# The seventh batch's norm, choice and places moved behind the last scores, the start reordered, two batches' sends two steps earlier

## The reference

```python
x = x + attn_a(layernorm(x))   # x: 8 x 256 x 128; 16 heads of 64, relative bias, full rows
x = x + ffn(layernorm(x))      # router over 8 experts, top 1
x = x + attn_b(layernorm(x))   # 64 x 32 tokens, low-rank keys and values, causal
x = x + ffn(layernorm(x))
# ffn:
router_logits = xt @ Wr + br
gates = max(softmax(router_logits)); idx = argmax(softmax(router_logits))
h = relu(layernorm(xt)*ln_g + ln_b through W1[idx] + b1[idx])
y = (h through W2[idx] + b2[idx]) * gates
```

## Time and profile before

| | |
|---|---|
| median of 3 runs | 656.47 us (655.35 to 656.65) |
| the profiled execution | 655.51 us |
| its span, first to last instruction | 654.2 us |
| mean granted clock of TensorE | 0.997 of 2.4 GHz |
| TensorE busy | 629.4 us, 96% |
| VectorE busy | 513.5 us, 78% |
| ScalarE busy | 529.0 us, 81% |
| GpSimd busy | 355.7 us, 54% |

### The profile page before, as it was taken

One profiled execution on the slowest core, in us unless ns is written; L12 is line 12 of the kernel. 1 busy time (PEld: TensorE's weight loads), 2 busy tenths in 40 slices (PEclk: granted clock), 3 DMA queues, 4 the chain that ended last, 5 costly groups with the idle time before them and its releaser, 6 DMA issues.

```text
span 654.2 us, 22111 instructions
## 1 busy us (share of the span) xinstructions
PE 629.4 (96%) x7454; PEld 537.3 (82%) x7454; DVE 513.5 (78%) x2211; ACT 529.0 (81%) x1776; POOL 355.7 (54%) x669
## 2 busy tenths in 40 slices
PE   6899999999999999989999999999999999989997
PEld 5578788788878788779997788888888888878997
DVE  4886878778987888988856687787888789888833
ACT  3888888879788878785665998898989898985664
POOL 4463545455465556743106564565657665762746
PEclk9999999999999999999999999999999999998999
DMA  8999989999980000133631100000000000112140
GB/s 271 284 321 326 273 229 326 330 329 289 286 238 10 11 2 26 42 100 91 168 96 37 34 3 3 8 2 7 6 7 19 12 11 2 50 52 74 49 132 19
DMA packets 90319, 74.78 MB, mean 114 GB/s; under 512 B 12225, under 2 KB 87111, under 8 KB 90080
## 3 DMA queue, kind: packets, MB, share of 16 engines
q1 hardware_dynamic: 86512, 66.24, 34.9%
q0 software_dynamic: 2848, 6.33, 3.0%
q10 hardware_dynamic: 848, 0.79, 0.5%
HBM read 19.93 MB, written 54.00 MB: 113 GB/s over the span
## 4 chain that ended last, share of the span: by engine, by line
PE 82%; issue 4%; DVE 4%; ACT 4%; POOL 3%; DMA 1%; SPq 0%; DVEq 0%; ACTq 0%; POOLq 0%
PE ps L558 17%; PE ps L671 14%; PE ps L715 13%; PE ps L553 10%; PE ps L554 8%; PE ps L555 8%; PE ps L821 5%; PE ps L837 5%; ACT ring L1020 2%; POOL out L439 1%; POOL ring L419 1%; DVE ring L1335 1%; DMA wkn<-in_w_qkv 1%; POOL xs_scratch L406 1%; PE ps L771 1%
## 5 line engine op out<-in xcount | busy, mean ns | idle before, releaser
L419 POOL TENSOR_SCALAR ring<-ring,rs 128x256 f32<-128x256 f32 (+1 forms) x500 | 218.8, 456 | 132.3 <-DVE rs L1347 130.9
L1020 ACT ACTIVATE ring<-ring,mn 128x256 f32<-128x256 f32 (+1 forms) x512 | 243.5, 482 | 5.8 <-DVE mn L1335 5.7
L558 PE MATMUL ps<-ident,ring 128*128 128x128 f32 x896 | 121.8, 275 | 4.8 <-DVE ol L1307 2.5
L558 PEld LDWEIGHTS ps<-ident,ring 128*128 128x128 f32 x896 | 102.0, 143 | 13.5 <-issue 4.7
L671 PE MATMUL ps<-qk 64*64 64x256 f32 (+1 forms) x2048 | 112.3, 356 | 0.6 <-ACT qk L992 0.4
L715 PE MATMUL ps<-pt,v 64*64 64x256 f32 (+3 forms) x2048 | 103.5, 340 | 1.5 <-ACT pt L1008 1.5
L1020 ACT ACTIVATION_READ_ACCUMULATOR ring<-ring,mn 128x1 f32 x512 | 101.3, 198 | 0.0
L715 PEld LDWEIGHTS ps<-pt,v 64*64 64x64 f32 x2048 | 75.3, 134 | 28.2 <-ACT pt L1008 6.0
L1362 DVE COPY pt<-ps 128x512 f32<-128x512 f32 (+1 forms) x128 | 75.5, 590 | 22.4 <-PE ps L558 21.0
L671 PEld LDWEIGHTS ps<-qk 64*64 64x64 f32 x2048 | 65.8, 132 | 29.0 <-issue 11.4
L992 ACT COPY qk<-ps 128x512 f32<-128x512 f32 x128 | 74.3, 580 | 9.9 <-PE ps L555 9.8
(11 more groups left out here) (209 smaller groups left out, 1298.0 us busy)
## 6 DMA issues: line engine op xcount, KB each, us to landing
xs_scratch<-f_ys SPq DMA_DIRECT2D x16, 2064.0 KB, 20.5
yr_scratch<-f_ys SPq DMA_DIRECT2D x8, 1024.0 KB, 10.6
f_xs<-xs_scratch SPq DMA_DIRECT2D x50, 129.0 KB, 2.3
w<-in_W SPq DMA_DIRECT2D x16, 256.0 KB, 5.9
xs_scratch<-f_ys SPq DMA_DIRECT2D x2, 1677.0 KB, 19.9
yr_scratch<-f_ys SPq DMA_DIRECT2D x25, 64.0 KB, 1.8
T<-in_bias SPq DMA_DIRECT2D x2, 512.0 KB, 7.9
T<-in_bias SPq DMA_DIRECT2D x1, 1024.0 KB, 10.4
```

The lines of the kernel that those rows point to most:

```text
L419: i = pool.tensor_scalar(part, part, rs[:, q], 1.0, ALU.mult, ALU.mult)
L558: return pe.transpose(out, src, ident[:, :])
L1020: i = act.activation(part, part, ACT.Exp, bias=mn[:, q], scale=-1.0, accum_out=sm[:, q])
```

## The change

Batch 6 leaves the common table and gets NEXT_POST: its sums stand in step 64 in place of 61, its logits and choice in 68, its places in 70; batch 7 keeps its steps 68 to 72. At the start of stage 1 ScalarE makes the value weights ahead of T(1) and does T(2) ahead of the first exponential; VectorE does products(3) and the norm of batch 1 in step 2, behind the first four scores, and its transposes come in step 5; GpSimd turns the bias tables a step off from before. Batches 1 and 3 are put up for sending before the step's send and not after it, so their first send comes one even step earlier. In step 63 VectorE does keep(58) between the reciprocal and the product of weigh(61), and index(4) behind S(63). The core of the diff:

```diff
+SENDS = {56: 2, 59: 2, 60: 2}
+BIASES = {1: 2, 2: 4, 4: 6}
+FIRST_PRE = {"a": 2, "a2": 4, "b": 5}
+NEXT_POST = {"sums": 64, "pow": 64, "a": 65, "xn": 65, "b": 66, "c": 68, "lg": 68, "choose": 68, "gate": 69, "d": 69, "place": 70}
...
+    if s == NEXT_POST[part]:
+        return NB - 2
     b = at(s, POST[part])
-    return b if b is not None and CALM <= b < NB - 1 else None
+    return b if b is not None and CALM <= b < NB - 2 else None
...
-            for _ in range(2 if s > 56 else 1):
-                if to_send and s <= NU and (s % 2 == 0 or s > 56):
+            if (b := calm_post(s, "place")) in ROUTED:
+                to_send.extend((j, ROUTE_NO[b], b) for j in range(*ROUTED[b]))
+            for _ in range(SENDS.get(s, 1 - s % 2)):
+                if to_send and s <= NU:
                     send()
-            for b in either(s, "place"):
-                to_send.extend((j, ROUTE_NO[b], b) for j in range(*ROUTED.get(b, (0, 0))))
+            if (b := post_at(s, "place")) in ROUTED:
+                to_send.extend((j, ROUTE_NO[b], b) for j in range(*ROUTED[b]))
                 while to_send and b >= NB - 2:
                     send()
...
+            if st == 0 and s == 1:
+                value_weights()
             if 0 <= s < NU:
                 T(s)
+            if s == 2:
+                expo(0, ALL[0])
             if st == 0 and s == 1:
-                value_weights()
                 products(3)
...
-                if s in (NU - 3, NU - 1):
+                if s == NU - 3:
                     weigh(s - 2)
                 if s == NU - 1:
+                    weigh(s - 2, (0,))
                     keep(NU - 6)
+                    weigh(s - 2, (1,))
                     TR(NU - 4)
                     TR(NU - 3)
+                S(s)
+                if s == NU - 1:
                     index(4)
-                S(s)
...
+            if s == NEXT_POST["sums"]:
+                sums(NB - 2)
+            if s == NEXT_POST["a"]:
+                post_a(NB - 2)
+                post_a2(NB - 2)
```

More of the change, by code:

```diff
@@ L104, in pre_at @@
         return 0 if st else None
+    if not st and part in FIRST_PRE:
+        if s == FIRST_PRE[part]:
+            return 1
+        if at(s, PRE[part]) == 1:
+            return None
     if st and s == PRE_1.get(part):
@@ L454, in step @@
                 weigh(s - 3)
-            if st == 0 and s in (1, 3, 5):
-                biases(s + 1)
-            if (b := pre_at(s + 1 if st and s < 0 else s - 1, "a", st)) is not None and (b or s < 0) and not (st and b == 1):
+            if st == 0 and s in BIASES:
+                biases(BIASES[s])
+            if st == 0 and s == FIRST_PRE["a"]:
+                pool_pow(rstd, half[:, 0:2], v_var0, p_pow0, 2)
+            if (b := pre_at(s + 1 if st and s < 0 else s - 1, "a", st)) is not None and (b or s < 0) and b != 1:
                 if st and b == 0:
@@ L758, in post_b @@
         def post_b(b):
-            PX = spare(("p", B0 + b), a_pTs, B0 + b + 1)
+            PX = spare(("p", B0 + b), a_pTs, B0 + b + 1, 3 if b == NB - 2 else None)
             pe.wait_ge(v_ph, B0 + b + 1)
@@ L765, in post_c @@
         def post_c(b):
-            PX = spare(("lg", B0 + b), v_lg, B0 + b + 1)
+            PX = spare(("lg", B0 + b), v_lg, B0 + b + 1, 3 if b == NB - 2 else None)
             pe.wait_ge(a_pTs, B0 + b + 1)
@@ L877, in step @@
                 TR(s - 4)
-            if post_at(s, "b") == NB - 2:
-                post_b(NB - 2)
+            if (b := post_at(s, "b")) is not None and b < NB - 2:
+                post_b(b)
             if s == max(LAST):
@@ L919, in after @@
         def after(s):
-            for b in either(s, "b"):
-                if b < NB - 2:
-                    post_b(b)
+            if (b := calm_post(s, "b")) is not None:
+                post_b(b)
+            if post_at(s, "b") == NB - 2:
+                post_b(NB - 2)
             for b in either(s, "c"):
@@ L1111, in step @@
                 keep(s - 6)
-            if s % 2 == 0 and 2 <= s < NU:
+            if s % 2 == 0 and 4 <= s < NU:
                 expo(s - 2, ALL[0])
+            if st == 0 and s == 1:
+                value_weights()
             if 0 <= s < NU:
                 T(s)
+            if s == 2:
+                expo(0, ALL[0])
             if st == 0 and s == 1:
-                value_weights()
                 products(3)
@@ L1161, in after @@
         def after(s):
-            for b in either(s, "b"):
-                if b < NB - 1:
-                    post_b(b)
+            if (b := calm_post(s, "b")) is not None:
+                post_b(b)
+            if post_at(s, "b") == NB - 2:
+                post_b(NB - 2)
             for b in either(s, "gate"):
@@ L1339, in S, with weigh @@
                 i.then_inc(v_mn, 1)
-        def weigh(u):
+        def weigh(u, parts=(0, 1)):
             U = U0 + u
             ring, sm, rs = a_ring[U % 4], a_sm[U % 4], a_rs[U % 4]
[L1344 to L1348, removed]
+            if 0 in parts:
+                dve.wait_ge(a_ex, U0 + u + 1)
+                if U >= 4:
+                    dve.wait_ge(p_nrm, U0 + u - 3)
+                dve.reciprocal(rs[:, :], sm[:, :]).then_inc(v_rs, 1)
+            if 1 in parts and nrm1_by_dve(u):
                 dve.wait_ge(v_rs, U0 + u + 1)
@@ L1557, in step @@
                 value_weights()
-                products(3)
             if s % 2 == 0 and 6 <= s < NU:
@@ L1564, in step @@
                 pre_c(b)
+            if st == 0 and s == FIRST_PRE["a2"]:
+                pre_a2(1)
             for v in VALUES[st].get(s, ()):
                 values(*v)
+            if st == 0 and s == FIRST_PRE["a"]:
+                products(3)
+                pre_a(1)
             if (b := at(s, 13)) is not None and b < NB - 1:
@@ L1594, in step @@
                 sums(b)
-            if (b := pre_at(s, "a2", st)) is not None and (st or b != 1):
+            if st and (b := pre_at(s, "a2", st)) is not None:
                 pre_a2(b)
@@ L1599, in step @@
                 S(s - 1)
[L1600 to L1603, removed]
-                if s in (NU - 3, NU - 1):
+                if s == NU - 3:
                     weigh(s - 2)
                 if s == NU - 1:
+                    weigh(s - 2, (0,))
                     keep(NU - 6)
+                    weigh(s - 2, (1,))
                     TR(NU - 4)
                     TR(NU - 3)
+                S(s)
+                if s == NU - 1:
                     index(4)
-                S(s)
             if s % 2 and 3 <= s < NU and s not in (NU - 3, NU - 1):
                 weigh(s - 2)
-            if (b := pre_at(s, "a", st)) is not None and (st or b != 1):
+            if st and (b := pre_at(s, "a", st)) is not None:
                 pre_a(b)
```

## The result

The changed kernel took 662.25 us (median of 11 runs, 660.45 to 666.11) against 656.19 us for the kernel before (11 runs, 655.35 to 659.11). The ratio is 1.0096, with a 95% interval of 1.0078 to 1.0114: 6 us, or 1%, slower. The prediction was 659.1 us with a range of 654.8 to 661.6. It had the direction and half of the size; the measured time lies 0.65 us above the range.

A forecast was written before the change was run, and what follows sets the result against it. TensorE, which hardly waits, was taken to bound the kernel, except at stage 2's end, which follows the gather. Terms −1.6 − 0.2 + 2.0 + 1.75 − 0.1 + 1.3 = +3.15 us on about 656.0 gave 659.1 us, range 654.8 to 661.6.

The forecast's parts named there:

- The start: Start of stage 1: waits for `wvh` and `qk` go and VectorE gets 1.8 us; −1.6 us, bounds 0 and −2.3.
- The sends: Earlier sends: −0.2 us in stage 1; in stage 2 a `ring` wait goes but TR(53) is 0.9 us late, −0.1 us.
- The last scores of stage 1: Stage 1, steps 61 to 63: xn(6) ahead of weigh(63) makes TR(63) late; +2.0 us, bounds +0.6 and +3.1.
- The rest of stage 1: Behind stage 1's last projection: VectorE's added 3.0 us for batch 6 delay the gather; +1.75 us, bounds +0.9 and +2.9.
- Stage 2's last scores: End of stage 2's scores: shorter causal weighs, so TR(63) not later, and the last projection about 0.9 us earlier.
- The clock: TensorE at half clock after waits, about 1.6 us per slow stretch; possible in stage 1, either sign, left out of the sum.
- The end of stage 2: Batch 6's places, sends and outputs ahead of batch 7's sends: 2.2 us later; with the 0.9 earlier, +1.3 us.
- Rival 3: A second slow-clock stretch in stage 1 after the wait at TR(63), 1.6 us more: 660.7 us; chance 0.13.
- Rival 1: Faster: with `row` before about 296, xn(6) fits ahead of weigh(63) and TR(63) isn't late; 654.1 us, chance 0.2.
- rival 2: Effects cancel: one of the two large terms at its low bound, the other halved; about +0.3, 656.3 us, chance 0.17.

The follow-up runs named there:

- e1_start: The kernel before with only the change's new order at the start of stage 1; 653.74 us, ratio 0.9963 to the kernel before.
- e2_sends: The kernel before with only the earlier sends of batches 1 and 3; 655.99 us, ratio 1.0002 to the kernel before.
- e10_xn_only: The changed kernel with only batch 6's xn moved behind weigh(63) on GpSimd, its power still ahead of weigh(62); 657.51 us, ratio 1.0025 to the kernel before.
- e9_vector_load: e4_no_b6 with idle VectorE copies, 7 and 9, where the changed kernel has batch 6's choice and places; 658.58 us, ratio 1.0054 to the kernel before.
- e6_behind_weighs: The changed kernel with GpSimd's power and xn of batch 6 one step later, behind weigh(62) and weigh(63); 657.44 us, ratio 1.0024 to the kernel before.
- e5_only_b6: The kernel before with only batch 6 moved, with its transposes' order and banks; 663.61 us, ratio 1.0128 to the kernel before.
- e4_no_b6: The changed kernel's start, sends and step 63, with batch 6 in its old steps; 652.87 us, ratio 0.9950 to the kernel before.
- e8_ahead_of_last: e6_behind_weighs with batch 6's logits and choice in step 66 and places in step 67; 662.22 us, ratio 1.0082 to the kernel before.

## Why the prediction was half right

**The start** was forecast at −1.6 us and brought −2.4 (e1_start, −3.4 to −1.5, so the forecast isn't excluded by it); the traces' means say −2.3. The mechanism was the right one: the wait of 1.13 us for `wvh` went, and so did the wait for T(2). If the term was too small, it is because part of the 1.8 us was to come back at pre_b(1): TensorE waits 0.56 us there, where it had waited 1.00 us before the `won` transposes.

**The sends** were forecast at −0.2 and −0.1 us, and e2_sends measures 0 (−0.9 to +1.1), too wide to tell. TR(53) was forecast 0.9 us late and is 0.93 us late in the changed kernel, but the place was read wrong: both weighs stand behind the send, so TensorE already waits at TR(52), 0.46 us, and in e2_sends it is less.

**The last scores of stage 1**: forecast +2.0 us against the start's and the sends' shift. Measured at TR(63), −0.45 against the −2.25 of the first PV in the same trace, this is +1.8. The term is right in size and in place (xn(6), then weigh(63)). The 0.5 us that it sees at TR(62) beside it are shown by e10_xn_only to be worth next to nothing.

**The rest of stage 1**: forecast +1.75; measured from TR(63) to the first transposes of stage 2, 1.98 + 0.45 = +2.4 us. The cause is in the main the one given, VectorE's added 3.0 us (at the rate of e9_vector_load they make 1.9 of the 2.4). Of 3.0 us hardly more than 0.6 were hidden. VectorE went from 13.87 to 14.62 us busy in the same 16 us, and its idle time was not where batch 7's chain could use it. By chance two errors, −0.65 at the start and +0.7 here, cancelled: stage 2 was forecast to begin at +1.95 and began at +1.98. That the first half of the sum came out is luck in this measure.

**Stage 2's last scores** are the step that failed: the wait for xn(6) ahead of weigh(63) was priced in stage 1 and put at nothing here. The prediction said: "Causal units need shorter weighs, so TR(63) is not later, and the removed waits make the last projection about 0.9 us earlier." The half weigh that is left for GpSimd there takes 1.06 us against 1.17 in stage 1, which is hardly shorter. And the weigh's length isn't what TR(63) waits for: the weigh stands behind xn(6), which waits for `row` until 597.58. TensorE's waits at TR(62) and TR(63) are 1.14 and 1.79 us, the same as in stage 1 (1.10 and 1.75). The half of the sentence on the removed waits held: PV(60) is 1.10 us earlier against the stage's own start. But TR(63) is 0.54 us late against it, and the last projection's sums 3.65 − 1.98 = 1.67 us, where −0.9 was forecast.

**The clock** comes on top in stage 2 of the profiled execution. The sums of the last projection are another 1.13 us later than TR(63) is, and in between lie the window at 0.50 and the matmuls of 1.89 us. These and PV(62) (2.09 us against 1.32) take 1.6 us more than at full clock; about 0.4 us of that comes back because TensorE no longer waits 0.42 us for `ol` ahead of the last projection. In e6_behind_weighs and e10_xn_only the wait at TR(63) is gone and the clock stays at 1.00. That alone doesn't show the wait to be the cause: e5_only_b6 has it too (0.89 and 1.79 us) and stays at 1.00, and so does stage 1 of the changed kernel (1.10 and 1.75 us). e1_start and e2_sends have the very waits of the kernel before in stage 2, and only one of them the slow stretch:

```profile
585.48 0.52 PE L568 MATMUL ps<-ident,ring 128*128 128x128 f32 x3 [0.91 <-DVE ol L1320]
587.76 1.32 PE L725 MATMUL ps<-pt,v 64*64 64x256 f32 x32 [0.63 <-ACT pt L1018]
```

```profile
586.26 0.52 PE L561 MATMUL ps<-ident,ring 128*128 128x128 f32 x3 [0.91 <-DVE ol L1310]
588.54 2.41 PE L718 MATMUL ps<-pt,v 64*64 64x256 f32 x32 [0.63 <-ACT pt L1011]
```

The same waits were followed by the fall in one execution and not in the other, so the length of the waits alone doesn't decide it, and what does was not settled. The mean granted clock of an execution was 0.997 or less in 7 of 11 of the changed kernel, in 4 of 6 of e5_only_b6, in 1 of 12 of e6_behind_weighs and in none of 12 of e10_xn_only: the wait at TR(63) seems to make the fall more frequent. The prediction put the rule of the Trainium skill ("TensorE: Matmul & The Clock Gate", Part 1: an idle TensorE falls to half clock) beside its sum and not into it, and it expected the fall, if any, in stage 1. The falls all came behind idle time of TensorE, as the rule has it, but e1_start, e5_only_b6 and stage 1 show as much idle time without one.

**The end of stage 2**: from the last projection to the gather 2.2 us were forecast and 6.16 − 3.65 = 2.5 came. Together with the two points above the term was −0.9 + 2.2 = +1.3 in the forecast. The trace has 6.36 − 1.98 = +4.4 us from the start of stage 2 to the last outputs. That is the whole of the miss: 3.1 us. In terms of the sum, 2.6 of them are the last scores and the projection of stage 2 (−0.9 forecast, +1.67 measured), of which the slow stretch is about 1.1, and 0.5 are the end.

**The rivals.** Rival 3 had the price of a slow stretch right (1.6 us forecast, 1.6 seen in the matmuls), in the wrong stage. Rival 1 hung on `row` before 296, in the kernel before's times. It came at 294.7 in stage 1, which with the start's shift of 2.25 us is 297.0 in those times. So the condition wasn't met, and the prediction's 297.5 was nearly right. But its idea is right in another form, as e4_no_b6 shows: with batch 6 in its old place the rest of the change is worth 3.3 us. Two of the prediction's sums don't come out: rival 2, as it is worded, gives +0.9 to +1.3 and not +0.3, and rival 3 with the upper bound of stage 2 gives 661.4 and not 661.6.

## What to carry to other kernels

A piece that leaves a crowded stretch takes its instructions on the other engines along. Here the work moved off the score steps was VectorE's, and most of what it cost came from two GpSimd instructions of 0.7 and 1.0 us (xn) that waited, at the head of GpSimd's queue, for VectorE, with a weigh behind them that TensorE needed. Before such a move, list for each engine the first instruction behind the moved one and ask who waits for that; then a one-step shift on that engine alone can win back most of the loss (4.7 of 6.3 us here). Where a reading holds for one stage, do the same sum with the numbers of the other stage, and don't wave it through on a shape.

## What the runs showed of the hardware

The granted clock of TensorE was at 0.50, which is 1.2 GHz, in some stretches behind waits: 0.91 and 0.63 us in the kernel before and in e2_sends, 1.14 and 1.79 in the changed one, 2.53 in e8_ahead_of_last. It stayed at 1.00 behind 0.91 and 0.63 us in e1_start, 0.89 and 1.79 in e5_only_b6, and 1.10 and 1.75 in stage 1 of the changed kernel. The same 32 matmuls of PV took 2.41 us in such a stretch and 1.32 outside. In e2_sends the six executions with a mean granted clock of 0.997 have a median of 657.1 us and the six at 1.000 one of 655.4.

Nine tiny copies of 128 x 8 on VectorE, each waiting for the one ahead, took 2.68 us in stage 1 of e9_vector_load where nine such steps of the routing take about 1.7. Seven of them took 0.16 to 0.17 us. The other two ran beside GpSimd's two instructions of xn, and each ended 0.03 us after one of these:

```profile
308.94 0.68 DVE L1684 COPY pad_v<-run 128x8 f32<-128x8 f32 x1
...
309.85 0.54 DVE L1684 COPY pad_v<-run 128x8 f32<-128x8 f32 x1
...
308.90 0.68 POOL L483 TENSOR_TENSOR row<-row,lng 128x256 f32<-128x256 f32 x1 [3.31 <-DVE row L1239]
309.66 0.69 POOL L486 TENSOR_TENSOR row<-row,lnb 128x256 f32<-128x256 f32 x1
```

Stage 2 shows the same (0.68 and 0.54 us beside xn). No run moved xn away to show that it is the cause.
